# Attention scores of two heads on the two halves of the array, and the causal mask added inside VectorE's maximum

## The reference

```
q, k, v = xn @ w + b, split into 16 heads of 8 channels     (attention a; b alike)
q, k    = rotary(q), rotary(k)
att     = softmax(where(causal, q @ k.T / sqrt(8), -inf))
x       = x + (att @ v, heads joined) @ wp + bp
q, k    = xn @ Wq, xn @ Wk, split into 8 heads of 64         (mixture)
v       = per head a sigmoid-weighted sum of the 2 best of 5 experts' values
x       = x + sum over the 2 best experts of (softmax(q @ k.T / 8) @ v) @ Wo
```

## Time and profile before

| | |
|---|---|
| median of 3 executions | 2207.96 us (2207.55 to 2214.34) |
| the profiled execution, its own time | 2209.6 us |
| its span, first to last instruction | 2207.9 us |
| TensorE busy (matmuls) | 1899.7 us, 86% |
| VectorE busy | 1637.4 us, 74% |
| ScalarE busy | 1275.3 us, 58% |
| GpSimd busy | 1045.1 us, 47% |
| mean granted TensorE clock | 0.945 |

### The profile page before, as it was taken

The page is one execution under the profiler, slowest core; times in us unless marked ns, Lnnn a source line. Parts: engine busy times, 40 slices in busy tenths (PEclk is TensorE's granted clock), DMA queues, the critical chain, the costliest instruction groups (busy, mean ns, idle before and its releaser), DMA issues.

```text
span 2207.9 us, 40511 instructions
## 1 busy us (share of the span) xinstructions
PE 1899.7 (86%) x11328; PEld 913.1 (41%) x11328; DVE 1637.4 (74%) x2950; ACT 1275.3 (58%) x2803; POOL 1045.1 (47%) x1124
## 2 busy tenths in 40 slices
PE   1758998899898889989888998989899898998775
PEld 0323444435354443535444353544434354443433
DVE  4548787877878787787878777787877777796561
ACT  0326657575665757566575756657575665757452
POOL 1214455462635546263554626355462635555433
PEclk8779999999999999999999999999999999999977
DMA  3121212020121202012120201212020121200000
GB/s 95 42 34 30 34 40 35 28 34 17 34 34 40 34 28 35 16 35 33 40 34 28 36 16 36 31 40 34 28 37 21 34 28 39 34 6 13 10 10 5
DMA packets 87623, 68.19 MB, mean 31 GB/s; under 512 B 10720, under 2 KB 83104, under 8 KB 87328
## 3 DMA queue, kind: packets, MB, share of 16 engines
q1 hardware_dynamic: 87456, 66.62, 16.5%
HBM read 32.51 MB, written 10.49 MB: 19 GB/s over the span
## 4 chain that ended last, share of the span: by engine, by line
PE 49%; DVE 29%; issue 12%; ACT 5%; DMA 2%; POOL 1%; DVEq 1%; SPq 0%; ACTq 0%; POOLq 0%; PEldq 0%; PEld 0%
DVE nmaxA L878 6%; PE Y L488 6%; PE S1c L429 4%; DVE ztmp L999 4%; DVE nmaxF L883 4%; PE S1b L429 4%; PE S2a L453 4%; PE M L619 3%; PE S2b L453 3%; PE Y L479 3%; PE S1a L429 3%; DVE rotated L924 2%; PE M L539 2%; ACT Pq L713 2%; PE M L592 2%
## 5 line engine op out<-in xcount | busy, mean ns | idle before, releaser
L1117 POOL TENSOR_TENSOR Z<-Z,ztmp 128x1280 f32<-128x1280 f32 x112 | 324.8, 2900 | 374.7 <-DVE ztmp L999 373.5
L1084 POOL TENSOR_SCALAR_AFFINE_SELECT PT<-PT 128x256 f32<-128x256 f32 (+1 forms) x640 | 248.3, 400 | 395.8 <-ACT PT L698 393.1
L1108 POOL TENSOR_TENSOR Vf<-Vf,ztmp 128x512 f32<-128x512 f32 x256 | 352.5, 1377 | 139.9 <-DVE ztmp L973 134.8
L698 ACT ACTIVATE PT<-S2a 128x512 f32<-128x512 f32 x320 | 191.1, 597 | 152.7 <-PE S2a L447 124.4
L488 PE MATMUL Y<-PT,Vf 128*64 128x512 f32 x1024 | 274.8, 617 | 0.0
L429 PE MATMUL S1a<-Kf,Qf 64*128 64x512 f32 x352 | 216.6, 698 | 6.6 <-ACT Pq L713 4.6
L973 DVE TENSOR_TENSOR ztmp<-xv,wv_s 128x512 f32<-128x512 f32 x256 | 219.7, 858 | 2.8 <-POOL Z L1117 2.8
L429 PE MATMUL S1c<-Kf,Qf 64*128 64x512 f32 x352 | 209.2, 676 | 12.6 <-ACT Pq L713 11.2
L702 ACT ACTIVATE PT<-S2a 128x512 f32<-128x512 f32 x256 | 153.1, 598 | 89.8 <-PE S2a L453 89.6
L698 ACT ACTIVATE PT<-S2b 128x512 f32<-128x512 f32 x320 | 191.3, 598 | 14.1 <-PE S2b L447 13.2
L429 PE MATMUL S1b<-Kf,Qf 64*128 64x512 f32 x320 | 190.8, 678 | 6.5 <-ACT Pq L713 6.5
(11 more groups left out here) (109 smaller groups left out, 3931.5 us busy)
## 6 DMA issues: line engine op xcount, KB each, us to landing
Qs<-parts SPq DMA_DIRECT2D x96, 128.0 KB
Ks<-parts SPq DMA_DIRECT2D x96, 128.0 KB
tab_s<-in_tab SPq DMA_DIRECT2D x16, 512.0 KB, 4.3
xr<-out_x SPq DMA_DIRECT2D x32, 256.0 KB, 2.8
out_x<-res SPq DMA_DIRECT2D x32, 256.0 KB, 2.2
wa_s<-in_wa SPq DMA_DIRECT2D x16, 320.0 KB, 2.9
xl<-out_x SPq DMA_DIRECT2D x16, 256.0 KB, 2.8
out_x<-in_x SPq DMA_DIRECT2D x8, 256.0 KB, 4.7
```

The lines of the kernel that those rows point to most:

```text
L698: nc.scalar.activation(PT[:, slot % 2, b, :], t[:, :], ACT.Exp, scale=SCALE_A).then_inc(exps_done.sem, 1)
L1084: last = nc.gpsimd.affine_select(out=v, in_=v, compare_op=ALU.is_ge, fill=0.0, base=0, pattern=pattern, channel_multiplier=-1)
L1108: nc.gpsimd.tensor_tensor(Vf[:, i, :, :], Vf[:, i, :, :], vtmp[:, n % VBUF, :, :], ALU.add).then_inc(v_acc.sem, 1)
L1117: nc.gpsimd.tensor_tensor(Z[:, :, :, :], Z[:, :, :, :], ztmp[:, hh % 2, :, :, :], ALU.add).then_inc(z_acc.sem, 1)
```

## The change

- Heads go in pairs of an even and an odd one. Qs and Ks hold eight head pairs; the even head's 48 product rows and two maximum rows are partitions 0 to 49, the odd head's 64 to 113. A score matmul takes 48 rows (first pass) or 50 (second).
- Both passes issue two banks at a time, one per head of the pair (the last two banks hold pieces of both pairs, again one bank even, one odd). The first pass waits, as the mixture's did, until two of its three banks are free; the second pass until both of its two are.
- The mask matmuls and the bfloat16 mask are gone. A float32 mask `maskw`, 128 x 512, zero but for the last 128 columns, is added by VectorE in `tensor_tensor_reduce`: score plus mask, written back to the bank, and the maximum of it. It reads PSUM and SBUF. It is one instruction per piece, 16 a group, each followed by an instruction that reads the accumulator. The maxima are no longer negated there, but in `split_maxima`.
- The scatter is 24 DMAs with half the pieces each, and the order of the weights' columns and the rotary tables is changed on the host to fit.

```diff
...
     NSP = len(SPLITS_Q)
-    ROWS_P1 = 96
+    ROWS_P1 = NSP * DA
     ROWS_P2 = ROWS_P1 + 2
+    HALF = 64
...
     BANKS_A2 = []
-    for pair in range(GA // 2):
-        h0, h1 = 2 * pair, 2 * pair + 1
-        for h in (h0, h1):
-            BANKS_A1 += [[(h, 3, 0)], [(h, 2, 0), (h, 0, 384)]]
-            BANKS_A2 += [[(h, 0, 0)], [(h, 1, 0), (h, 3, 384)]]
-        BANKS_A1.append([(h0, 1, 0), (h1, 1, 256)])
-        BANKS_A2.append([(h0, 2, 0), (h1, 2, 256)])
+    for h0 in range(0, GA, 2):
+        BANKS_A1 += [[(h, 3, 0)] for h in (h0, h0 + 1)] + [[(h, 2, 0), (h, 0, 384)] for h in (h0, h0 + 1)]
+        BANKS_A2 += [[(h, 0, 0)] for h in (h0, h0 + 1)] + [[(h, 1, 0), (h, 3, 384)] for h in (h0, h0 + 1)]
+    BANKS_A1 += [[(h, 1, 0), (h + 2, 1, 256)] for h in (0, 1)]
+    BANKS_A2 += [[(h, 2, 0), (h + 2, 2, 256)] for h in (0, 1)]
     NA_B = len(BANKS_A1)
...
         identb = sb("identb", [P, P], BF)
-        maskb = sb("maskb", [P, P], BF)
+        maskw = sb("maskw", [P, T])
         wa_s = sb("wa_s", [P, 5, C])
...
         parts = sb("parts", [P, 2, 3, T], BF)
-        Qs = sb("Qs", [ROWS_P2, HA, T], BF)
-        Ks = sb("Ks", [ROWS_P2, HA, T], BF)
+        Qs = sb("Qs", [P, HA // 2, T], BF)
+        Ks = sb("Ks", [P, HA // 2, T], BF)
         Vs = sb("Vs", [P, NT, HA, DA + 1])
-        nmaxA = sb("nmaxA", [P, HA, NT])
-        nmb = sb("nmb", [P, 2, GA, NT], BF)
+        maxA = sb("maxA", [P, 2, HA // 2, NT])
+        nmb = sb("nmb", [P, 2, 2, GA // 2, NT], BF)
         mrowA = sb("mrowA", [2 * GA * NT, P], BF)
...
                     apart(sp)
-                    for i in range(2):
-                        sp.dma_start(Qs[ROWS_P1 + i:ROWS_P1 + i + 1, GA * group:GA * group + GA, :],
-                                     mrowA[i * GA * NT:(i + 1) * GA * NT, :]).then_inc(rowsA_in.sem, 16)
+                    for odd in range(2):
+                        r = HALF * odd + ROWS_P1
+                        sp.dma_start(Qs[r:r + 2, GA // 2 * group:GA // 2 * (group + 1), :],
+                                     mrowA[odd * GA * NT:(odd + 1) * GA * NT, :]).then_inc(rowsA_in.sem, 16)
...
                         for r in range(NSP):
-                            sp.dma_start(dst[DA * r:DA * r + DA, :, :],
-                                         parts[:, qk, order[r], :]).then_inc(scattered.sem, 16)
+                            for lo in (0, HALF):
+                                sp.dma_start(dst[lo + DA * r:lo + DA * r + DA, :, :],
+                                             parts[lo:lo + HALF, qk, order[r], :]).then_inc(scattered.sem, 16)
...
                     t = S1[(n - 1) % len(S1)]
-                    if group >= SA and b % GF:
+                    if b % 2:
                         return
...
                     if group == 0 and b == 0:
-                        pe.wait_ge(scattered.sem, scattered.at(j, 2 * NSP))
+                        pe.wait_ge(scattered.sem, scattered.at(j, 4 * NSP))
                     if group == SA and b == 0:
                         pe.wait_ge(*drained(j, "F k3", 1))
-                    pe.wait_ge(*s1_free(j, (n if group < SA else n + 1) - len(S1)))
+                    pe.wait_ge(*s1_free(j, n + 1 - len(S1)))
                     if group < SA:
-                        for h, qt, col in BANKS_A1[b]:
-                            hh, keys = GA * group + h, (qt + 1) * P
-                            nc.tensor.matmul(t[:, col:col + keys], Qs[0:ROWS_P1, hh, qt * P:keys],
-                                             Ks[0:ROWS_P1, hh, 0:keys], start=True, stop=False)
-                            last = nc.tensor.matmul(t[:, col + qt * P:col + keys], identb[:, :], maskb[:, :],
-                                                    start=False, stop=True)
-                        last.then_inc(s1_filled.sem, 1)
+                        for i in range(2):
+                            for h, qt, col in BANKS_A1[b + i]:
+                                hh, keys, r = GA * group + h, (qt + 1) * P, HALF * (h % 2)
+                                last = nc.tensor.matmul(S1[(n - 1 + i) % len(S1)][:, col:col + keys],
+                                                        Qs[r:r + ROWS_P1, hh // 2, qt * P:keys],
+                                                        Ks[r:r + ROWS_P1, hh // 2, 0:keys], start=True, stop=True)
+                            last.then_inc(s1_filled.sem, 1)
                     else:
...
                     t = S2[(n - 1) % len(S2)]
+                    if slot < SA and b % 2:
+                        return
                     if not (a if slot < SA else f):
...
                         pe.wait_ge(rowsA_in.sem, rowsA_in.at(j, 2 * slot + 2, 1))
-                    pe.wait_ge(exps_done.sem, exps_done.at(j, n - len(S2)))
+                    pe.wait_ge(exps_done.sem, exps_done.at(j, (n + 1 if slot < SA else n) - len(S2)))
                     if slot < SA:
-                        for h, kt, col in BANKS_A2[b]:
-                            hh = GA * slot + h
-                            last = nc.tensor.matmul(t[:, col:col + T - kt * P], Ks[0:ROWS_P2, hh, kt * P:kt * P + P],
-                                                    Qs[0:ROWS_P2, hh, kt * P:T], start=True, stop=True)
+                        for i in range(2):
+                            for h, kt, col in BANKS_A2[b + i]:
+                                hh, r = GA * slot + h, HALF * (h % 2)
+                                last = nc.tensor.matmul(S2[(n - 1 + i) % len(S2)][:, col:col + T - kt * P],
+                                                        Ks[r:r + ROWS_P2, hh // 2, kt * P:kt * P + P],
+                                                        Qs[r:r + ROWS_P2, hh // 2, kt * P:T], start=True, stop=True)
+                            last.then_inc(s2_filled.sem, 1)
                     else:
                                                        ident[:, :])
-                    last.then_inc(s2_filled.sem, 1)
+                        last.then_inc(s2_filled.sem, 1)
...
             nc.vector.memset(Ks[:, :, :], 0.0).then_inc(dve_init.sem, 1)
+            nc.vector.memset(maskw[:, 0:T - P], 0.0).then_inc(dve_init.sem, 1)
             nc.vector.memset(Y[:, :], 0.0).then_inc(dve_init.sem, 1)
             nc.vector.memset(minus_half[:, :], -0.5).then_inc(dve_init.sem, 1)
-            dve.wait_ge(dve_init.sem, 5)
-            nc.vector.memset(Ks[ROWS_P1:ROWS_P2, :, :], 1.0).then_inc(dve_init.sem, 1)
+            dve.wait_ge(dve_init.sem, 6)
+            for lo in (0, HALF):
+                nc.vector.memset(Ks[lo + 32:lo + HALF, :, :], 1.0).then_inc(dve_init.sem, 1)
             dve.wait_ge(dve_init.sem, dve_init.per)
...
                     if group < SA:
-                        segs = BANKS_A1[b]
-                        h0, qt0, _ = segs[0]
-                        if len(segs) == 2 and segs[1][1] == qt0:
-                            last = nc.vector.tensor_reduce(nmaxA[:, GA * group + h0:GA * group + h0 + 2, qt0],
-                                                           t[:, :].rearrange("p (h k) -> p h k", h=2), AX.X, ALU.max,
-                                                           negate=True)
-                        else:
-                            for h, qt, col in segs:
-                                last = nc.vector.tensor_reduce(nmaxA[:, GA * group + h, qt:qt + 1],
-                                                               t[:, col:col + (qt + 1) * P], AX.X, ALU.max, negate=True)
+                        apart(dve)
+                        for h, qt, col in BANKS_A1[b]:
+                            keys = (qt + 1) * P
+                            last = nc.vector.tensor_tensor_reduce(
+                                t[:, col:col + keys], t[:, col:col + keys], maskw[:, T - keys:T], 1.0, -3.0e38,
+                                ALU.add, ALU.max, maxA[:, h % 2, GA // 2 * group + h // 2, qt:qt + 1])
                         last.then_inc(s1_read.sem, 1)
...
                     dve.wait_ge(*filled(j, f"rows{before}", 1 if group == 1 else 0))
-                    src = nmaxA[:, GA * group:GA * group + GA, :]
-                    nc.vector.tensor_copy(nmb[:, 0, :, :], src).then_inc(maxA_chain.sem, 1)
+                    src = maxA[:, :, GA // 2 * group:GA // 2 * (group + 1), :]
+                    nc.vector.tensor_scalar(nmb[:, :, 0, :, :], src, -1.0, None, ALU.mult).then_inc(maxA_chain.sem, 1)
                     dve.wait_ge(maxA_chain.sem, maxA_chain.at(j, group + 1, lag))
-                    nc.vector.tensor_tensor(nmb[:, 1, :, :], src, nmb[:, 0, :, :], ALU.subtract).then_inc(nmb_ready.sem, 1)
+                    nc.vector.scalar_tensor_tensor(nmb[:, :, 1, :, :], src, -1.0, nmb[:, :, 0, :, :], ALU.mult,
+                                                   ALU.subtract).then_inc(nmb_ready.sem, 1)
...
-    plain = [h * D + d for d in range(D) for h in range(H)]
-    swapped = [h * D + (d + D // 2) % D for d in range(D) for h in range(H)]
```

(2 more changed lines are left out.)

15 lines of the change are left out of this document (7 added, 8 removed).

## The result

The changed kernel takes **2336.28 us** (median of 4 runs, 2331.75 to 2337.59), the kernel before beside it on the same chip 2207.76: ratio 1.0574, 95% interval 1.0546 to 1.0602. It is slower by 128 us. The forecast was 2294 us in a range of 2175 to 2400: the side and the range held, and the loss was half as large again as forecast (86 us). As will be seen, it is also put together in another way.

What follows compares the result with a forecast made beforehand. VectorE was taken to pace slots 6, 7, 0 and 1, TensorE the other four. Terms of 4.9 + 0.5 = 5.4 us per period, times 16, gave 86 us; 2209.6 + 86 - 1.6 = 2294 us, range 2175 to 2400.

Steps and rivals of the forecast that it cites:

- the 3.8 of 12.4 us a period that TensorE saves: 64 mask matmuls per period, 3.8 us; with 8.5 from halves at best 12.4 saved, of which 10.2 lie under VectorE.
- VectorE sets the pace of slots 6, 7, 0 and 1: First-pass attention, 64.8 us of each 128.0 us period: VectorE busy 56.5 us and the bound; TensorE bounds the other four slots.
- Price of an item, 0.12 with its read 0.07: Added cost of each fused masked maximum on VectorE, including its accumulator read: 2.06 us per group, 8.2 us per period.
- the lower bound of 5.0 us a period: Least that the fused maxima were to add on VectorE, taking 0.07 us an item; the upper bound was 17.2.
- the first rival: Accumulator read hides in VectorE's overlap, costing 0.03 instead of 0.07 us: -2.9 us per period, 2162 us; chance 0.17.
- a read under 0.05 us: Sign that the prediction is wrong: VectorE's accumulator read, expected at 0.07 to 0.1 us, takes less than 0.05.
- Rival 4, half rate: Fused operation on VectorE takes two cycles an element: 21 us per period on top, 2630 us; chance 0.03.
- The three waits on TensorE, 3.3 us, can go: VectorE's waits of 1.10, 1.36 and 0.80 us for banks in slots 6, 7, 0 and 1 vanish: -3.3 us per period.
- The 2.49 us at the loop's turn stay: VectorE's gap at the loop's turn, which nothing in the profile released, was taken to remain unchanged.
- +0.5 us for the pairs in slots 2 and 3: Second-pass pairs close a chain of 3.57 us against 3.16; per period +0.5 us, bounds 2.1 saved to 3.3 lost.
- Rival 3, the clock: TensorE's clock falls once more per period, slowing matmuls of slot 1 or 2: +2 us, 2326 us; chance 0.07.
- The scatter: 24 DMAs instead of 12 cost SP 8.1 us more issuing; with 4.8 us of cover before slot 6, counted as nothing.

## Why the prediction was right, and where it was not

Each change of ratio along one row of kernels, times 2208 us; each differs from the one above it in one thing, but for the second step, which holds three:

| step | ratio | us | the prediction's term |
|---|---|---|---|
| before to no mask work | 1 to 0.9973 | -6 | the 3.8 of 12.4 us a period that TensorE saves |
| halves, new order, 24 transfers | to 1.0030 | +13 | under VectorE: 0 |
| first pass in pairs | to 0.9899 | -29 | with the masks, -3.3 a period of waits: -53 |
| second pass in pairs | to 1.0156 | +57 | +0.5 a period: +8 |
| fused maxima, loop moved | to 1.0385 | +51 | +8.2 a period: +131 |
| loop where it was | to 1.0574 | +42 | none |
| sum | | +127 | |

The order matters: with single banks the last two steps together cost 94 us, in the kernel before 75, with only the second pass single 99.

1. *VectorE sets the pace of slots 6, 7, 0 and 1.* Right for 7 and 0, shown from both sides: without the masks on TensorE they kept their length, and with the fused maxima in their place (second to third row of the table of slots) slot 7 took 1.2 us more and slot 0 3.1, of which 2.0 are the second gap. Slot 1 kept its length within 0.2 us in both, so it hangs on neither, and what sets it is open. Over the program 2.7 to 3.8 us more on VectorE cost 3.2 a period (51 / 16). Wrong for slot 6, where TensorE was busy for 18.49 of 18.50 us, where less work on it gave 0.5 us and where single halves cost 1.3. The prediction took four slots as one window; one by one they would have shown it. It also read that VectorE has no other gap over 0.4 us there; there is one of 1.1 us at the start of slot 6, a wait for GpSimd.
2. *Price of an item, 0.12 with its read 0.07.* **Over-sized.** The read costs nothing start to start, and an item comes to 2.7 / 64 = 0.04 to 3.8 / 64 = 0.06 us: under the lower bound of 5.0 us a period. This is the first rival's mechanism, past the 0.07 at which it was to decide, and a read under 0.05 us was one of the prediction's own signs of being wrong; that the kernel still became slower is due to the next steps. Rival 4, half rate, did not come: 512 columns take 0.62 us. The trace names the operation `CUSTOM_DVE_ANT_0`; that it belongs to the family whose rule the prediction quotes, no row shows.
3. *The three waits on TensorE, 3.3 us, can go.* **This step failed**, and not because the waits stayed. As a mean over eight units VectorE waits for first-pass banks 3.9 us a period before, 2.8 after and 1.2 with the loop moved; where only the pairs of the first pass differ it is 1.7 against 3.7 (second pass single, fused) and 1.4 against 4.3 (no mask work), so the pairs do shorten them. But two of the three, 2.5 of the 3.3 us, lie in slot 6, which TensorE sets: there they fell to 1.0 us, and the slot is as long as before. Taking out the masks and pairing the first pass brought 35 us, where 53 were counted on, and the halves took 13 of them back.
4. *The 2.49 us at the loop's turn stay.* They stayed, and a second gap came, 2.1 us by itself and 42 us with its effect on the clock. The prediction treated the gap as a constant of the kernel; it depends on where the loop lies.
5. *+0.5 us for the pairs in slots 2 and 3.* **Under-sized.** The mechanism is the one described, at 3.33 us a round instead of 3.57, but slots 2 and 3 together take 3.4 us more than before and 3.7 more than with single banks, just past the upper bound of 3.3. The chain was held against one round of slot 3, 3.16 us; in slot 2 the rounds were 2.71 and 2.74, so that slot, in which the prediction looked for less, pays as much as slot 3. That TensorE "has most other work between the pairs" did not help; its matmuls are queued behind the waiting pair. Slot 0, in which the second pass runs too, pays another 1.3.
6. *Rival 3, the clock.* It came true in kind, and larger. Per period the clock is at 0.50 for 24 us, where before it was for 6.4; the 4 us at 956 were part of a stretch of 6.8. The kernel with its second pass single still has 20 us and the fastest one here 12, so the low clock alone is not the loss.
7. *The scatter.* Right. 12 issues of one half take 8 us, no first score in the loop waits for a DMA, and slots 4 and 5 are as long as before:

```profile
1046.15 7.91 SPq L364 DMA_DIRECT2D Qs<-parts  x12
1058.16 8.08 SPq L364 DMA_DIRECT2D Ks<-parts  x12
```

So the sum of 86 us becomes the measured 127 to 128 by 80 less for the items, 31 more for masks, halves and first-pass pairs together (-22 in place of -53), 49 more for the pairs of the second pass and 42 for the second gap. The side was right in part for its reason, a dearer VectorE where it sets the pace; the size came near by luck, through errors of opposite sign. Without the second gap the kernel takes 2293 us, a microsecond from the forecast, and that is the same luck. What stays open: why the head-by-head order costs 29 us, why the first slot begins up to 12 us sooner in some kernels than in others, and how much of each step is the clock.

## What to carry to other kernels

Two edits in one change should be costed and tried apart: of this change the pairs of the first pass are worth keeping, and with the second pass single and no mask in the maximum they make 2183 us out of 2208 (of which 6 are the masks'). Here pairs paid with three banks and a consumer that was already behind, and cost with only two banks to go round, where the producer is next in a ring (scores, maximum, exponential, scores); a third bank for the second pass was not tried. Read busy time slot by slot: four slots in one window hid that one of them belonged to another engine. And look at a loop's turn in the profile of both kernels before reading anything else: a gap there that no wait explains can come or go with the number of instructions ahead of it.

## What the runs showed of the hardware

- A jump back to the loop's start stops VectorE for 1.9 to 2.8 us in every kernel here, 12 times each. That agrees with the Trainium skill (Runtime: NRT & Kernel Launch, Instruction fetch mechanics), by which a taken branch out of the fetched window waits for its target page. The same section calls the crossing of a block border mostly hidden; here the second stall of 1.9 to 2.25 us, just behind the turn, was not, and 64 instructions of padding ahead of the loop removed it. That the border of a fetched piece fell there is the reading that fits; the place of the border itself no view shows.
- The accumulator read behind a fused operation shows 0.14 us and takes none from the next instruction.
- Two matmuls on the two halves start in the same 0.01 us also for scores of 50 rows (1031.71 and 1031.71 above). The change into halves after transposes on the full array costs 0.10 us (0.53 against 0.43), and the change back to transposes as much (0.32 against 0.22); from the second pass's pair to the feed-forward pair, both on halves, 1031.93 - 1031.71 = 0.22 us pass for 512 columns, so it costs nothing there.
